# Hand-overs between the stages of a twelve-stage transformer kernel: starting at the last sum instead of the last norm

## The chip, the cores and the metric

One Trainium2 chip, one of its cores. The metric is the device time of one execution in microseconds (us), lower is better. The kernel of before ran three times: 4346.09, 4349.70 and 4349.97 us, median 4349.7. Another execution was recorded by the profiler.

## The reference, cut to what matters

A residual stream x of 2048 tokens by 256 channels (16 blocks of 128 tokens) passes twelve layers. Each computes

    x = layernorm(x + f(x))        # no scale, no shift

with another f: delta-rule attention, self attention, a spline layer, retention, quantized cross attention, a gated layer with 8-bit weights, latent attention, channel attention over a context, a ternary gated layer, a Mamba-2 scan, channel attention again, and an int8 layer. The ternary layer, whose order changes most, is

    xq = round(127 / max|n| * n) / (127 / max|n|),  n = rms_norm(x)
    p  = silu(xq @ sign(W_g).T) * (xq @ sign(W_u).T)
    f  = p @ sign(W_d).T

## The kernel before, in words

Every layer is a class (a stage), and x stays in SBUF all the time: `X` as 16 tiles of 128 tokens by 256 channels, and `xT`, its transpose, for the stages whose products need channels on the partitions. The stages are Delta, SelfAttention, Spline, Retention, Cross, Gated, Latent, Channels, Ternary, Scan, ChannelsGamma and Quant (n = 0 to 11). Tokens go through a stage in four groups of four blocks.

There is no scheduler. Each engine gets one long queue: stage after stage, and within a stage the steps that `order()` yields, so the order is written by hand. Engines meet by semaphores. `xn` counts groups whose norm has been written to X, `xt` counts halves of groups whose transpose has been kept in xT. `room[b]` names the event after which PSUM bank b is free.

A stage ends, for a group, with the sums (VectorE adds the product in PSUM to X and writes `R`), the norm (`norm_vector`: statistics L217 and L220, an inverse root in eleven small instructions L196 to L209, four scalings to X L241), the turn (`turn_tensor` L173: eight transposes on TensorE into two banks) and the copy to xT (`turn_scalar` L182, ScalarE). The norm's last scaling raises `xn`.

The next stage begins with `before(eng)` (L272), a wait for `over(n - 1)` (L188): all of xT kept if the stage in front is one that turns x (`TURNED`: Delta, Spline, Cross, Gated, Ternary), else all norms written. TensorE, ScalarE, VectorE and GpSimd call it. SelfAttention and Retention are without it on TensorE and have a step "last" in which they turn the last group of the stage in front. After it, TensorE sets all `room` to `over(n)`, so no bank is used earlier.

What the hand-overs look like on the engines:

- Cross (class at L1444): TensorE turns the context (ct), then k, v, then waits for VectorE's quantized weights (w) and rows (xq). GpSimd clears two tiles (`xVE`, L1813). VectorE: `w0`, `xq`, `v`.
- Gated (L1817): VectorE converts the weights `fgui` to `fgu` (L1905), GpSimd converts `fdni` to `fdn` in four instructions (L1929 to L1932), TensorE's first columns (L301) need `fgu`.
- Latent (L1935): TensorE multiplies weights with weights in steps "a" (L2010, four of them), then "dn" of group 0 (L307), the first step that reads xT.
- Channels (L2478): TensorE transposes the context, GpSimd makes `hXE` and `hKE` (L2693, L2696) after a small tile of VectorE (`hone`, L2634). Its last steps on VectorE are the products "mul" (L2658), behind ScalarE's copy hO (L2622). Channels can take steps of the stage behind it (`ASIDE`); before, only ChannelsGamma did this, for Quant.
- Ternary (L2714): ScalarE takes the signs of the weights (L2812, L2813). VectorE's "prep" normalizes a group, finds its largest values and rounds it to `tQB` (L2852 to L2866); then TensorE transposes (qt), and for every block u: "gu" (L2781, two banks each for gate and up), silu on ScalarE (L2826), the product on VectorE (L2873), "pt" (transposes, L2788), copies (L2831 on ScalarE, L2879 on VectorE), "dn" (L2799). In iteration t come gu of block t, pt of block t - 1, dn of block t - 2; prep of the next group at t = 1, 5, 9, sums and norm of the last one ("close") at t = 5, 9, 13, 17, the turn at t = 6, 10, 14, 18.
- Scan (L2887): TensorE multiplies dt for groups 0, 1 (n = 0) and 2, 3 (n = 1); ScalarE takes Abs of each (L3074), then Exp of each (L3078); VectorE's chain (L3141 on) follows. GpSimd builds tables (L3240 to L3257).
- ChannelsGamma (L2706): its context is loaded when the norm of Scan is over (`may_load`), because there is no room earlier.

Weights of a stage with `EARLY` are loaded one stage ahead, when `over(n - 2)` is reached.

Of the kernel before, what the change touches and what calls it, by code (L numbers as in the profile page):

```python
# [17 lines left out]
D = 256  # L18
# [227 lines left out]
class Stage:  # L246
# [926 lines left out]
class Retention(Stage):  # L1173
# [35 lines left out]

    def order(self):  # L1210
# [233 lines left out]
class Cross(Stage):  # L1444
# [37 lines left out]

    def order(self):
# [65 lines left out]
    def tensor(self, pe):  # L1549
        c, bank, room = self.c, self.c.bank, self.c.room  # L1550
        self.before(pe)
# [111 lines left out]
        for b in range(8):  # L1663
            room[b] = c.over(self.n)
# [53 lines left out]
    def vector(self, dve, own):  # L1718
        c, bank = self.c, self.c.bank
        self.before(dve)  # L1720
# [96 lines left out]
class Gated(Stage):  # L1817
# [18 lines left out]
    def buffers(self):  # L1836
# [3 lines left out]
        self.pj, self.dw, self.gs, self.hs = t("proj", 48), t("down", 4), s("silu", 24), v("h", 24)  # L1840
        self.wg, self.wd = v("w", 2), p("w", 1)

    def order(self):
# [8 lines left out]
        yield "turn", 3, 0  # L1852

    def tensor(self, pe):
        c, bank, room = self.c, self.c.bank, self.c.room
        for step, g, n in self.order():
# [11 lines left out]
            elif step == "dn":  # L1868
# [3 lines left out]
                for b in range(4):  # L1872
# [6 lines left out]
                    room[4 + b // 2] = c.xn.at(4 * self.n + g + 1)  # L1879
# [3 lines left out]
        for b in range(8):  # L1883
            room[b] = c.over(self.n)

    def scalar(self, act, own):
# [3 lines left out]
        for step, g, n in self.order():  # L1890
# [6 lines left out]
            elif step == "turn":  # L1897
                c.turn_scalar(act, self.n, g, (6, 7))

    def vector(self, dve, own):  # L1900
        c, bank = self.c, self.c.bank
        self.before(dve)
# [3 lines left out]
        for step, g, n in self.order():  # L1906
# [8 lines left out]
            elif step == "dn":  # L1915
                dve.wait_ge(*self.dw.at(g + 1))
                sums = [own(dve.tensor_tensor(c.R[:, x, :], bank(4 + x // 2)[:, blk(x % 2, 256)], c.X[:, 4 * g + x, :], ALU.add))
                        for x in range(4)]
                c.norm_vector(dve, own, self.n, g, sums)
# [15 lines left out]
class Latent(Stage):  # L1935
# [41 lines left out]

    def order(self):
# [3 lines left out]
        for step, g in shared(0):  # L1982
            yield step, g, 0, 0
        for n in range(4):
# [14 lines left out]
    def tensor(self, pe):  # L1999
        c, bank, room = self.c, self.c.bank, self.c.room  # L2000
        self.before(pe)
        pe.wait_ge(self.dma[1], 112)
        for step, g, u, e in self.order():
# [10 lines left out]
            elif step == "b":  # L2014
# [6 lines left out]
                room[2 + g] = self.bcs.at(g + 1)  # L2021
            elif step == "dn":
                if g == 0:
# [72 lines left out]
    def scalar(self, act, own):  # L2096
# [4 lines left out]
        for step, g, u, e in self.order():  # L2101
            s, gs = u % 4, g % 2
            if step == "a":
# [54 lines left out]
    def vector(self, dve, own):  # L2158
        c, bank = self.c, self.c.bank
        self.before(dve)  # L2160
# [316 lines left out]

class Channels(Stage):  # L2478
# [4 lines left out]
    PLACE, REST, GAMMA, LOADS = 57504, 80000, False, 5  # L2483
# [31 lines left out]

    def order(self):
# [16 lines left out]
    def tensor(self, pe):  # L2533
        c, bank, room = self.c, self.c.bank, self.c.room
        self.before(pe)
# [88 lines left out]
    def vector(self, dve, own):  # L2624
        c, bank = self.c, self.c.bank
        self.before(dve)
# [79 lines left out]
class ChannelsGamma(Channels):  # L2706
# [3 lines left out]
    def may_load(self, sp):  # L2710
        Stage.may_load(self, sp)


class Ternary(Stage):  # L2714


    PLACE, REST, EARLY, TURNED = 0, None, True, True

    def weights(self):
        c = self.c  # L2720
        self.gu, self.gub = c.f32("tgu", 2, 2, 1024), c.at("tgub", [128, 2, 2, 1024], BF16)
        self.dn = c.f32("tdn", 8, D)

    def load(self, sp):
        i = self.ins
        self.may_load(sp)
        cp = lambda a: a.rearrange("(c p) n -> p c n", p=128)
        self.fetch(sp, 0, (self.gu[:, 0, :, :], cp(i["t_gu"][0])), (self.gu[:, 1, :, :], cp(i["t_gu"][1])), (self.dn[:, :, :], cp(i["t_dn"])))

    def buffers(self):  # L2730
        c = self.c
        self.XN, self.s8, self.sw, self.m = (c.sets(2, "t" + n, *z) for n, *z in (("XN", 4, D), ("st", 4, 8), ("sw", 12), ("m", 12)))
        self.QB = [c.at(f"tQB{i}", [128, 4, D], BF16) for i in range(2)]
        self.QT = [c.at(f"tQT{i}", [128, 2, 512], BF16) for i in range(2)]
        self.G, self.PM, self.PT = c.sets(2, "tG", 512), c.sets(2, "tPM", 1024), c.sets(2, "tPT", 8, 128)
        t, s, v = ((lambda name, n, e=e: self.sig(e, name, n)) for e in ("tensor", "scalar", "vector"))
        self.qt, self.gm, self.um, self.pt, self.dw = t("qt", 4), t("g", 32), t("u", 32), t("pt", 32), t("dn", 16)
        self.ws, self.qtc, self.gs, self.pca = s("w", 3), s("qt", 4), s("silu", 32), s("pt", 16)
        self.iv, self.qb, self.pm, self.pcv = v("scale", 4), v("q", 4), v("p", 32), v("pt", 16)

    def order(self):
        yield "prep", 0, 0
        yield "qt", 0, 0
        for t in range(19):
            for h in range(2):
                if t < 16:
                    yield "gu", t, h
                if 0 <= t - 1 < 16:
                    yield "pt", t - 1, h
            if t % 4 == 1 and t < 12:  # L2750
                yield "prep", t // 4 + 1, 0
            if t % 4 == 3 and t < 12:
                yield "qt", t // 4 + 1, 0
            if t % 4 == 2 and t > 4:
                yield "turn", t // 4 - 1, 0
            if 0 <= t - 2 < 16:
                yield "dn", t - 2, 0
            if t % 4 == 1 and t > 4:
                yield "close", t // 4 - 1, 0

    def tensor(self, pe):
        c, bank, room = self.c, self.c.bank, self.c.room
# [695 lines left out]
```

## Time and profile before

| | before |
|---|---|
| time, median of 3 runs | 4349.7 us |
| the profiled execution | 4350.02 us, span 4348.2 us |
| TensorE busy | 3718.2 us (86%) |
| VectorE busy | 3160.9 us (73%) |
| ScalarE busy | 1977.4 us (45%) |
| GpSimd busy | 966.3 us (22%) |
| mean granted TensorE clock | 0.918 |

PE is TensorE's matmuls, PEld its weight loads, DVE VectorE, ACT ScalarE, POOL GpSimd. The span is from the first to the last instruction of the profiled execution; times in rows are counted from its start. A granted clock of 1.00 is 2.4 GHz, of 0.50 it is 1.2 GHz, and a value between is the mean of a stretch at both. In a row of instructions, "[7.04 <-DVE X L241]" says that the engine had been idle for 7.04 us and that the idle time ended with an instruction of VectorE, line 241, that writes X. With "x8" the row holds eight instructions one after the other, and the time is that of all.

### The profile page before, as it was taken

How to read it: one execution, taken by the hardware profiler on the slowest of the kernel's cores; microseconds unless marked ns; L12 is line 12 of the kernel's file. 1: busy time of each engine (PE TensorE's matmuls, PEld its weight loads, DVE VectorE, ACT ScalarE, POOL GpSimd, SP SyncE). 2: the span in 40 equal slices, each digit the busy share in tenths (PEclk: the TensorE clock that was granted, in tenths of full speed). 3: DMA queues.
4: the chain of work that ended last, by engine and by line, in shares of the span. 5: the costliest groups of instructions: out<-in, count | busy, mean ns of one | idle time of the engine just before them, and what ended most of it. 6: DMA issues, size and time to landing. Idle time of an engine off the chain costs nothing. (4 is left out here: it accounts for less than half of the span.)

```text
span 4348.2 us, 69549 instructions
## 1 busy us (share of the span) xinstructions
PE 3718.2 (86%) x25068; PEld 2252.3 (52%) x25068; DVE 3160.9 (73%) x7102; ACT 1977.4 (45%) x4701; POOL 966.3 (22%) x1237
## 2 busy tenths in 40 slices
PE   7799999998843868797999897769999999997985
PEld 3466666665522446554555554545555555554543
DVE  7789988897577665533556568558888888886678
ACT  4466666665511423212333234226556555563345
POOL 2433321354011000000111131023323233233220
PEclk9899999999965989897999989879999999997897
DMA  2222222222110000100000000200000000001000
GB/s 67 69 63 69 62 60 62 65 64 48 54 37 27 5 22 2 54 19 21 1 1 1 8 23 23 100 1 1 1 1 1 1 1 1 1 1 47 1 1 20
DMA packets 220707, 120.09 MB, mean 28 GB/s; under 512 B 115280, under 2 KB 213200, under 8 KB 219152
## 3 DMA queue, kind: packets, MB, share of 16 engines
q1 hardware_dynamic: 220368, 115.65, 9.6%
q8 instruction: 203, 3.33, 0.3%
q14 instruction: 136, 1.11, 0.1%
HBM read 100.89 MB, written 14.68 MB: 27 GB/s over the span
## 5 line engine op out<-in xcount | busy, mean ns | idle before, releaser
L301 PE MATMUL ps<-xT,min 128*128 128x512 f32 (+1 forms) x1072 | 534.8, 628 | 7.3 <-DVE mZ L3179 5.0
L3184 DVE SCALAR_TENSOR_TENSOR macc<-ps,mcw,macc 128x508 f32<-128x508 f32 (+2 forms) x408 | 302.9, 742 | 146.3 <-ACT macc L3108 136.7
L3122 ACT ACTIVATE mE<-ps,mcol 128x128 f32<-128x128 f32 x1024 | 291.3, 370 | 7.8 <-PE ps L3024 0.8
L301 PEld LDWEIGHTS ps<-xT,min 128*128 128x128 f32 (+1 forms) x1072 | 182.9, 191 | 191.1 <-issue 180.8
L3270 POOL TENSOR_TENSOR mE<-mE,mCB 128x512 f32<-128x512 f32 x128 | 163.7, 1279 | 481.5 <-ACT mE L3122 481.5
L3054 PE MATMUL ps<-mwo,macc 128*128 128x256 f32 x1024 | 246.0, 383 | 19.2 <-DVE macc L3218 19.2
L2616 ACT ACTIVATE hE<-ps 128x512 f32<-128x512 f32 x256 | 139.0, 594 | 223.2 <-PE ps L2578 223.2
L3277 POOL TENSOR_TENSOR mSQ<-mSQ,mtn 128x512 f32<-128x512 f32 x128 | 163.4, 1277 | 257.7 <-ACT mtn L3126 257.7
L2151 ACT ACTIVATE lP<-ps,lm 128x128 f32<-128x128 f32 x256 | 90.6, 366 | 266.1 <-DVE lm L2211 266.1
L3054 PEld LDWEIGHTS ps<-mwo,macc 128*128 128x128 f32 x1024 | 186.0, 191 | 47.3 <-DVE macc L3218 25.6
L2646 DVE TENSOR_REDUCE hMX<-ps 128x2 f32<-128x512 f32 x256 | 158.9, 684 | 60.2 <-PE ps L2557 60.2
L2242 POOL TENSOR_TENSOR lP<-lP,lm 128x512 f32<-128x512 f32 x64 | 66.6, 1041 | 578.3 <-DVE lm L2215 578.3
L723 DVE SCALAR_TENSOR_TENSOR dav<-ps,dsmall,dav 128x508 f32<-128x508 f32 (+2 forms) x192 | 142.4, 742 | 47.9 <-ACT dav L594 43.4
L817 POOL TENSOR_TENSOR dTB<-did,dNB 128x1024 f32<-128x1024 f32 (+1 forms) x10 | 28.7, 2866 | 663.7 <-DMA dNB<-d_N 599.5
L822 POOL TENSOR_TENSOR dTB<-dTB,dtmp 128x30 f32<-128x30 f32 (+11 forms) x300 | 169.1, 564 | 23.5
L2578 PE MATMUL ps<-hXE,hKE 32*128 32x256 f32 x1024 | 163.0, 440 | 12.7 <-DVE hXE L2652 7.2
L723 DVE SCALAR_TENSOR_TENSOR daq<-ps,dsmall,daq 128x508 f32<-128x508 f32 (+2 forms) x192 | 142.5, 742 | 39.1 <-ACT daq L594 33.6
L493 PE MATMUL ps<-dKQ 128*128 128x256 f32 x512 | 137.6, 395 | 28.6 <-ACT dO L669 19.2
L821 POOL TENSOR_TENSOR dtmp<-dNB,dTB 128x30 f32<-128x30 f32 (+11 forms) x300 | 155.2, 517 | 23.5
L723 DVE SCALAR_TENSOR_TENSOR dak<-ps,dsmall,dak 128x508 f32<-128x508 f32 (+2 forms) x192 | 142.3, 741 | 23.3 <-ACT dak L594 18.7
L3108 ACT ACTIVATE macc<-ps,ms,mcw 128x512 f32<-128x512 f32 x136 | 105.9, 779 | 115.0 <-PE ps L301 115.0
L2055 PE MATMUL ps<-lCQ,lq 128*128 128x512 f32 (+1 forms) x256 | 142.6, 656 | 17.7 <-DVE lQA L2206 17.7
(593 smaller groups left out, 8957.8 us busy)
## 6 DMA issues: line engine op xcount, KB each, us to landing
dwk<-in_L_attn_Wk SPq DMA_DIRECT2D x64, 128.0 KB, 2.3
dwq<-in_L_attn_Wq SPq DMA_DIRECT2D x64, 128.0 KB, 2.3
dwv<-in_L_attn_Wv SPq DMA_DIRECT2D x64, 128.0 KB, 2.4
dwg<-in_L_attn_Wg SPq DMA_DIRECT2D x64, 128.0 KB, 2.4
dwo<-in_L_attn_Wo SPq DMA_DIRECT2D x64, 128.0 KB, 2.6
min<-in_m_in SPq DMA_DIRECT2D x2, 4096.0 KB, 17.0
d_N<-dNT SPq DMA_DIRECT2D x256, 16.0 KB, 1.5
dTT<-d_TT SPq DMA_DIRECT2D x256, 16.0 KB, 1.9
```

The lines of the kernel that those rows point to most:

```text
L301: t = pe.matmul(out, w[:, j, :], self.c.xT[:, j, blk(g, 512)], start=j == 0, stop=j == 1)
L723: x = dve.scalar_tensor_tensor(out=acc[:, :, 3 - j:T], in0=p[:, :, 0:T - 3 + j], scalar=small[:, 4 * k + j:4 * k + j + 1], in1=acc[:, :, 3 ...
L821: then(pool.tensor_tensor(part, bc(NB[:, s, s + 1:32], s, True), bc(TB[:, s, 0:s], 31 - s), ALU.mult))
L822: then(pool.tensor_tensor(low, low, part, ALU.subtract))
L2055: t = pe.matmul(bank(b), w, self.CQ[gs][0:K, i, :], start=i == 0, stop=i == 1)
L2578: t = pe.matmul(bank(4 + i)[:, blk(lt, 256)], self.KE[x][r, e, blk(lt)], self.XE[x][r, e, :], start=True, stop=True)
L2646: m = dve.tensor_reduce(self.MX[y][:, k, 32 * r:32 * r + 32:16], bank(r).rearrange("p (e n) -> p e n", e=2), AX.X, ALU.max, negate=True)
L3054: t = pe.matmul(bank(j // 2)[:, blk(j % 2, 256)], self.acc[s][:, blk(j)], self.wo[:, i, :], start=i == 0 and j % 2 == 0, stop=i == 31 and ...
L3122: x = act.activation(self.E[s][:, e, blk(j)], bank(4 + e)[:, blk(j)], ACT.Exp, bias=self.col[:, 4 * g + j, 0, 2 * i + e:2 * i + e + 1])
L3184: x = dve.scalar_tensor_tensor(out=acc[:, :, 3 - j:T], in0=p[:, :, 0:T - 3 + j], scalar=self.cw[:, i, j:j + 1], in1=acc[:, :, 3 - j:T], op ...
L3270: pool.tensor_tensor(g4(self.E[s][:, 0, :]), g4(self.E[s][:, 0, :]), self.CB[g % 2][:, :, :], ALU.mult).then_inc(*self.m0.up)
L3277: pool.tensor_tensor(self.SQ[g % 2][:, :], self.SQ[g % 2][:, :], self.tn[s][:, :], ALU.add).then_inc(*self.sqa.up)
```

## The change

`before` waits for `ended()` of the stage in front. That is its last sums where the class says so (Retention, Cross, Gated, Latent, Channels, Ternary, Scan), else `over` as before. TensorE does not wait at all for the stage in front in Cross, Latent, Channels and Scan; VectorE waits for the norms (`xn`), not for xT.

```diff
     def before(self, eng):
-        eng.wait_ge(*self.c.over(self.n - 1))
+        eng.wait_ge(*(self.prev.ended() if self.prev else self.c.over(-1)))
...
+    def ended(self):
+        return self.c.over(self.n)
...
 class Cross / Latent / Channels / Scan
     def tensor(self, pe):
-        self.before(pe)
     def vector(self, dve, own):
-        self.before(dve)
+        dve.wait_ge(*self.c.xn.at(4 * self.n))
```

(Gated.vector has the same new wait; Scan.gpsimd has `pool.wait_ge(*c.xn.at(4 * self.n))` in place of `before`; Gated.gpsimd and Cross.gpsimd keep `before`, which is now `ended()` of Cross and of Retention.) Cross, Gated and Ternary no longer set every bank to `over`. The last group of Cross is turned by Gated, of Gated by Latent, of Ternary by Scan:

```diff
 class Cross
-                        for g in range(4):
+                        for g in range(3 if x == "turn" else 4):
...
 class Gated, order()
                 yield "h", g, n
+                if g == 0 and n == 1:
+                    yield "last", 3, 0
...
-        yield "turn", 3, 0
...
-                    room[4 + b // 2] = c.xn.at(4 * self.n + g + 1)
+                    room[4 + b // 2] = self.su.at(g + 1)
...
+            elif step == "last":
+                c.turn_tensor(pe, self.n - 1, g, (6, 7))
...
 class Latent, order()
         for step, g in shared(0):
             yield step, g, 0, 0
+            if step == "dn":
+                yield "last", 3, 0, 0
...
 class Scan, tensor() and scalar()
         for n in range(2):
+            if n:
+                c.turn_tensor(pe, self.n - 1, 3, (6, 7))
             pe.wait_ge(*room[n])
+            pe.wait_ge(*c.xt_ready(self.n, 2 * n + 1))
...
 class ChannelsGamma
     def may_load(self, sp):
-        Stage.may_load(self, sp)
+        sp.wait_ge(*self.prev.ended())
```

Ternary is moved ahead of Channels in the file, since Channels now takes two of its steps (`ASIDE = Ternary.BESIDE`), on VectorE alone. Prep is cut in two, "prep" (statistics, inverse root, scaling) and "round" (the rest), and sums and norm of a group are two steps:

```diff
+    BESIDE = {16: ("prep", 0), 17: ("round", 0)}
...
     def order(self):
-        yield "prep", 0, 0
         yield "qt", 0, 0
         for t in range(19):
             for h in range(2):
                 if t < 16:
                     yield "gu", t, h
                 if 0 <= t - 1 < 16:
                     yield "pt", t - 1, h
-            if t % 4 == 1 and t < 12:
-                yield "prep", t // 4 + 1, 0
+            if t % 4 < 2 and t < 12:
+                yield ("prep", "round")[t % 4], t // 4 + 1, 0
             if t % 4 == 3 and t < 12:
                 yield "qt", t // 4 + 1, 0
-            if t % 4 == 2 and t > 4:
+            if t % 4 == 3 and t > 4:
                 yield "turn", t // 4 - 1, 0
             if 0 <= t - 2 < 16:
                 yield "dn", t - 2, 0
             if t % 4 == 1 and t > 4:
                 yield "close", t // 4 - 1, 0
+            if t % 4 == 2 and t > 4:
+                yield "norm", t // 4 - 1, 0
...
-                room[6 + b // 2] = c.xn.at(4 * self.n + g + 1)
+                room[6 + b // 2] = self.su.at(g + 1)
             elif step == "turn":
-                c.turn_tensor(pe, self.n, u, (6, 7))
+                c.turn_tensor(pe, self.n, u, (4, 5))
...
     def scalar(self, act, own):
-        self.before(act)
         act.wait_ge(self.dma[0], 48)
         (signs of the weights)
+        self.before(act)
```

The semaphores of Channels are handed on for reuse one stage later than those of the others.

## Rows read from the trace of the kernel before

**Rows 1.** Stretches Gated, Ternary: length; busy PE, PEld, DVE, ACT, POOL; PEclk, DMA, GB/s.

```profile
1824.70:1971.80 147.10, 138.06 (x416) 72.41 (x416) 48.23 (x138) 22.15 (x33) 9.15 (x4) 0.96 0.18 53
...
2709.00:2876.30 167.30, 114.68 (x568) 86.66 (x568) 95.44 (x296) 44.38 (x62) 0.00 (x0) 0.84 0.20 79
```

**Rows 2.** Who waited for whom, Cross to Scan: us in total, times, longest.

```profile
PE ps L173 <- DVE X L241: 50.9, 6, 12.2
```

**Rows 3.** Timeline of DVE at Ternary's end: start, us, instruction, count [idle before].

```profile
2869.33 1.42 DVE L2882 TENSOR_TENSOR R<-ps,X 128x256 f32<-128x256 f32 x4 [6.22 <-PE ps L2799]
...
2874.90 1.38 DVE L241 TENSOR_SCALAR X<-R,st,rsq 128x256 f32<-128x256 f32 x4
```

**Rows 4.** Timeline at the start of Cross, POOL and PE.

```profile
1582.46 3.55 POOL L1813 MEMSET xVE<- 128x2048 f32 x2 [179.02 <-DVE X L241]
...
1594.78 1.23 PE L1539 MATMUL ps<-ident,cwr 128*128 128x128 f32 x8 [0.29 <-DVE xVE L1756]
```

**Rows 5.** Timeline at two places in Scan and Delta, DVE beside POOL.

```profile
2879.38 1.07 DVE L3167 CAST msel<-rsq 128x8 bf16<-128x8 f32 x1
...
2879.04 1.38 POOL L3240 MEMSET R<- 128x1536 bf16 x1 [206.05 <-ACT xT L182]
...
955.81 2.86 DVE L207 TENSOR_TENSOR dsw<-dsw 128x4 f32<-128x4 f32 x1
...
955.80 2.85 POOL L817 TENSOR_TENSOR dTB<-did,dNB 64x1024 f32<-64x1024 f32 x1 [23.06 <-DMA dNB<-d_N]
```

**Rows 6.** Timeline at the start of Gated, PE and POOL.

```profile
1828.40 3.72 PE L301 MATMUL ps<-xT,fgu 128*128 128x512 f32 x4 [1.69 <-DVE fgu L1905]
1832.46 26.33 PE L301 MATMUL ps<-xT,fgu 128*128 128x512 f32 x60 [0.33 <-DVE fgu L1905]
...
1827.42 4.14 POOL L1929 TENSOR_SCALAR fdn<-fdni 128x1280 f32<-128x1280 int32 x1 [241.41 <-ACT xT L182]
```

**Rows 7.** Timeline of PE at the start of Latent, and one stretch of it.

```profile
1971.86 1.97 PE L173 MATMUL ps<-ident,X 128*128 128x128 f32 x8 [7.04 <-DVE X L241]
1974.60 5.55 PE L2010 MATMUL ps<-lkvT,lqT 128*128 128x64 f32 x32 [0.77 <-ACT xT L182]
...
1974.60:1980.00 5.40, 5.40 (x32) 5.24 (x32) 0.00 (x0) 0.59 (x1) 0.00 (x0) 0.50 0.00 0
```

**Rows 8.** Timeline of POOL at the start of Channels.

```profile
2497.89 0.94 POOL L2693 TENSOR_SCALAR hXE<-X,hpar 128x256 f32<-128x256 f32 x2 [16.28 <-DVE hone L2634]
```

**Rows 9.** Timeline from Channels to Ternary, DVE, ACT and PE.

```profile
2694.32 1.75 DVE L2658 RECIPROCAL hO<-hO 128x256 f32<-128x256 f32 x1 [5.97 <-ACT hO L2622]
...
2700.63 1.75 DVE L2658 RECIPROCAL hO<-hO 128x256 f32<-128x256 f32 x1 [3.64 <-ACT hO L2622]
...
2718.29 0.69 DVE L2866 TENSOR_SCALAR tQB<-tXN 128x1024 bf16<-128x1024 f32 x1
...
2708.99 3.71 ACT L2812 ACTIVATE tgub<-tgu 128x2048 bf16<-128x2048 f32 x2 [8.39 <-DVE X L241]
...
2721.24 5.22 PE L2781 MATMUL ps<-tgub,tQT 128*128 128x512 bf16 x12 [1.10 <-ACT tQT L2820]
```

**Rows 10.** Timeline inside Ternary, PE and DVE; L2781 begins an iteration.

```profile
2747.84 1.03 PE L2781 MATMUL ps<-tgub,tQT 128*128 128x512 bf16 x4
...
2774.90 1.94 PE L173 MATMUL ps<-ident,X 128*128 128x128 f32 x8 [12.19 <-DVE X L241]
...
2788.84 1.03 PE L2781 MATMUL ps<-tgub,tQT 128*128 128x512 bf16 x4
...
2794.89 1.03 PE L2781 MATMUL ps<-tgub,tQT 128*128 128x512 bf16 x4
...
2755.30 0.75 DVE L2873 SCALAR_TENSOR_TENSOR tPM<-ps,tm,tG 128x512 f32<-128x512 f32 x1 [3.35 <-PE ps L2781]
```

**Rows 11.** Timeline of ACT at the start of Scan, the second Abs.

```profile
2884.87 0.69 ACT L3074 ACTIVATE mCB<-ps,mh 128x512 f32<-128x512 f32 x1 [1.33 <-PE ps L301]
```

**Rows 12.** Timeline of DVE at the start of ChannelsGamma.

```profile
3991.74 0.23 DVE L2629 TENSOR_REDUCE hrow<-ident 128x1 f32<-128x4 f32 x2 [4.42 <-DMA hctx<-in_ctx]
```

More of the change, by code:

```diff
@@ L1208, in buffers, with ended @@
         self.vz = p("v_zero", 1)
+    def ended(self):
+        return self.sm.at(8)
     def order(self):
@@ L1481, in buffers, with ended @@
         self.vz = p("v_zero", 1)
+    def ended(self):
+        return self.sum.at(4)
     def order(self):
@@ L1662, in tensor @@
                 c.turn_tensor(pe, self.n, g, (0, 1))
-        for b in range(8):
-            room[b] = c.over(self.n)
     def scalar(self, act, own):
@@ L1840, in buffers, with ended @@
         self.pj, self.dw, self.gs, self.hs = t("proj", 48), t("down", 4), s("silu", 24), v("h", 24)
+        self.su = v("sum", 4)
         self.wg, self.wd = v("w", 2), p("w", 1)
+    def ended(self):
+        return self.su.at(4)
     def order(self):
@@ L1882, in tensor @@
                 c.turn_tensor(pe, self.n, g, (6, 7))
-        for b in range(8):
-            room[b] = c.over(self.n)
+            elif step == "last":
+                c.turn_tensor(pe, self.n - 1, g, (6, 7))
     def scalar(self, act, own):
@@ L1898, in scalar @@
                 c.turn_scalar(act, self.n, g, (6, 7))
+            elif step == "last":
+                c.turn_scalar(act, self.n - 1, g, (6, 7))
     def vector(self, dve, own):
         c, bank = self.c, self.c.bank
-        self.before(dve)
+        dve.wait_ge(*self.c.xn.at(4 * self.n))
         dve.wait_ge(self.dma[0], 96)
@@ L1916, in vector @@
                 dve.wait_ge(*self.dw.at(g + 1))
-                sums = [own(dve.tensor_tensor(c.R[:, x, :], bank(4 + x // 2)[:, blk(x % 2, 256)], c.X[:, 4 * g + x, :], ALU.add))
-                        for x in range(4)]
-                c.norm_vector(dve, own, self.n, g, sums)
+                for x in range(4):
+                    o = dve.tensor_tensor(c.R[:, x, :], bank(4 + x // 2)[:, blk(x % 2, 256)], c.X[:, 4 * g + x, :], ALU.add)
+                o.then_inc(*self.su.up)
+                dve.wait_ge(*self.su.at(g + 1))
+                c.norm_vector(dve, own, self.n, g, [0] * 4)
     def gpsimd(self, pool, own):
@@ L1976, in buffers, with ended @@
         self.pn = p("pn", 64)
+    def ended(self):
+        return self.su.at(4)
     def order(self):
@@ L2000, in tensor @@
         c, bank, room = self.c, self.c.bank, self.c.room
-        self.before(pe)
         pe.wait_ge(self.dma[1], 112)
@@ L2021, in tensor @@
                 room[2 + g] = self.bcs.at(g + 1)
+            elif step == "last":
+                c.turn_tensor(pe, self.n - 1, g, (4, 5))
             elif step == "dn":
+                pe.wait_ge(*c.xt_ready(self.n, g))
                 if g == 0:
@@ L2102, in scalar @@
             s, gs = u % 4, g % 2
+            if step == "last":
+                c.turn_scalar(act, self.n - 1, g, (4, 5))
+                continue
             if step == "a":
@@ L2159, in vector @@
         c, bank = self.c, self.c.bank
-        self.before(dve)
+        dve.wait_ge(*self.c.xn.at(4 * self.n))
         dve.wait_ge(self.dma[0], 48)
@@ L2478 @@
 class Channels(Stage):
-    PLACE, REST, GAMMA, LOADS = 57504, 80000, False, 5
+    PLACE, REST, GAMMA, LOADS, ASIDE = 57504, 80000, False, 5, Ternary.BESIDE
     def weights(self):
@@ L2514, in buffers, with ended @@
         self.xe, self.ke, self.ve = p("xe", 16), p("ke", 16), p("ve", 16)
+    def ended(self):
+        return self.sum.at(16)
     def order(self):
@@ L2625, in vector @@
         c, bank = self.c, self.c.bank
-        self.before(dve)
+        dve.wait_ge(*self.c.xn.at(4 * self.n))
         dve.wait_ge(self.dma[0], 32)
@@ L2936, in buffers, with ended @@
         self.sq0, self.m0, self.sqa = p("sq0", 4), p("m", 128), p("sq", 128)
+    def ended(self):
+        return self.summed.at(4)
     def order(self):
@@ L3072, in scalar @@
         for n in range(2):
+            if n:
+                c.turn_scalar(act, self.n - 1, 3, (6, 7))
             act.wait_ge(*self.dm.at(n + 1))
@@ L3129, in vector @@
         c, bank = self.c, self.c.bank
-        self.before(dve)
+        dve.wait_ge(*self.c.xn.at(4 * self.n))
         dve.wait_ge(self.dma[0], 80)
@@ L3238, in gpsimd @@
         c = self.c
-        self.before(pool)
+        pool.wait_ge(*c.xn.at(4 * self.n))
         zero = own(pool.memset(self.spread[:, :, :, :, :], 0.0))
@@ L3288, in program @@
             stages.append(kind(core, n))
-            if not stages[n].ASIDE:
-                core.hand_on(stages[n])
+            for m in (n - 1, n):
+                if m >= 0 and bool(stages[m].ASIDE) == (m < n):
+                    core.hand_on(stages[m])
         with nc.Block() as block:
```

322 lines of the change are left out of this document (168 added, 154 removed).

## The prediction

> **What bounds the kernel now.** I read the table by stage first: TensorE is busy 94% of Gated and 69% of Ternary [rows 1]. So most of the time is TensorE's own work, which the change leaves alone; what it can win lies where TensorE stands still. The list of waits gives the common cause: the turns of x (L173) waited 50.9 us in six waits for the norm (L241), the longest 12.2 us [rows 2]. A hand-over is a chain: the sums end, the norm follows, then the turn, its copy, and the next stage. From the end of the last sums of Ternary (2870.75) to the end of the norm (2876.28) it is 5.5 us [rows 3]; call that one norm. Times are start us, and the engine at each one must be asked what it waited for *last*.
>
> **Retention to Cross.** TensorE, ScalarE and the two memsets of xVE begin one norm earlier. But VectorE's own chain (its norm, w0, xq, then v) runs unbroken into the turn of the weights, which waited for xVE, 0.29 us [rows 4]: TensorE's early start wins 0. The memsets do not come free. Rows of two other places show GpSimd holding up VectorE: a CAST of 8 elements took 1.07 us and ended with a memset, and a 4-element product took 2.86 us beside a GpSimd instruction of 2.85 us [rows 5]. The memsets, 3.55 us from 1576.8 on, now lie on the norm, whose small tensor_scalars come at 1578.6, as the second one starts: +1.75 us (bounds 0 and 1.8).
>
> **Cross to Gated.** Undisturbed, VectorE converts fgu right after the norm (1824.7 instead of 1827.36), so the first columns start at 1825.8 instead of 1828.40; the last turn, about 1 us at full speed, now lies inside a stage where TensorE is full: -3 + 1 = -2.0. But GpSimd's four instructions (9.15 us busy, some of it waiting [rows 1]; 4.14 us the first [rows 6]) also start one norm earlier, at 1817.86, just behind the bias add, and then alternate with the norm's small instructions. GpSimd, 7.7 us without its waits, ends at 1827.3; VectorE still owes the products and the scaling, 3 us: norm end at 1830.3 instead of 1824.68. Columns start at 1831.3, the second group (at half clock the first takes 3.72) at 1835.0 instead of 1832.46 [rows 6]: +2.5, and +1.0 for the turn: **+3.5 us**. Bounds -2.0 (GpSimd never blocks) and +5.5 (the clock rises later too). The Trainium skill (SBUF, State Buffer, section Who interferes with whom) has the rule that speaks against this move: the shared ports are a lock, and the later of the two engines blocks entirely. These rows agree; by it the sum stays as it is.
>
> **Gated to Latent.** TensorE idled 7.04 us before the turn at 1971.86, so it was free at 1964.8; the products "a" (two runs like the one shown, 11 us) began at 1974.60 [rows 7], then dn(0). Both read loaded weights and x turned earlier, so after the change "a" starts at 1964.8: -9.8 us. The last turn falls after dn(0), where TensorE waits for VectorE anyway: 0. Further, "a" ran at a granted clock of 0.50 [rows 7] behind the idle time; now it follows full-clock work with no gap. If it stayed full, "a" would take 5.5: another 5.5 saved. But the same row shows TensorE busy for all of 5.4 us with the clock not rising, so this narrow work (64 columns) does not hold the clock well; I take half, 2.7. **-12.5 us**, bounds -9.8 and -15.3. By the Trainium skill (TensorE: Matmul & The Clock Gate, section The HAM clock gate), what counts is how busy the engine has been, and "a" would stay full throughout; the rows at 0.50 speak against it.
>
> **Latent to Channels.** The first scores wait for GpSimd's hXE, which waits for VectorE's hone [rows 8], behind the norm as before. 0 (bounds 0.3 either way).
>
> **Channels to Ternary.** VectorE does prep and round of group 0 inside Channels. Prep is statistics, root and scaling, as the norm: 5.6 us; both end 10.0 us after the norm (2708.96 to 2718.98) [rows 9], so round is 4.4. Prep fits the idle 5.97 us, round has 3.64 us [rows 9]: norm end +0.7, at 2709.7. The signs (3.71 us, and 1.9 for tdn) start at 2700.6 behind the last hO; tQT is copied by 2707.3; columns start at 2707.4 instead of 2721.24 [rows 9]: -13.8.
>
> **Inside Ternary.** One iteration at full speed is 6.05 us; four were 41.0 (2747.84 to 2788.84), since prep, sums and norm (17 us on VectorE) stood in one block and the turn waited 12.19 us [rows 10]. Per iteration VectorE owes two products (0.75 [rows 10]) and a copy, 2.0 us, so it can spend 4.0 more before it falls behind, and TensorE runs one iteration ahead. In three blocks (prep 5.6; round and sums 5.8; norm 5.6) I get, from the start A of the iteration with prep: VectorE done at A+9.6, then A+17.4, while dn of the next group, due at A+14.7, waits for those sums: 2.7 lost. The turn is due at A+23.9; its first bank waits for the qt copy, the second, bank 5, for the copy of pt behind the norm, A+26.9: 2.6 lost beside 1.7 of turn and qt. 24.2 + 2.7 + 2.6 + 1.3 = 30.8, and 0.9 for a clock that sags in such gaps: 31.7 instead of 41.0, twice: -18.6. In the first four iterations prep costs 3.5 instead of 5.5, with the clock -2.0. After the last group's sums the norm stalls 2.6 instead of 4.5 (with the clock, -3.5). **Ternary in all -37.9**; bounds -13.8 (the hand-over alone) and -43 (no stall left).
>
> **Ternary to Scan.** dt of groups 0, 1 runs before the turn and Abs(0) after the sums. Abs(1) then stands where Abs(0) stood, so what lies between them goes: 1.33 + 0.69 [rows 11] = **-2.0** (bounds -1.0, and -2.7, the turn with its copy). GpSimd's tables come earlier by the same.
>
> **Scan to ChannelsGamma.** The context is fetched from the sums on, not the norm; VectorE idled 4.42 us for it [rows 12]. It lands before the norm ends: **-4.4**. SP has Quant's loads behind it, also earlier, not needed for 40 us. Loads of Latent wait for the moved turn in Gated, some us later, 130 us ahead of need: 0. The semaphores handed on later cost nothing.
>
> **Sum.** 1.75 + 3.5 - 12.5 + 0 - 37.9 - 2.0 - 4.4 = -51.6. The profiled execution took 4350.02 us (span 4348.2), 0.3 above the median of 4349.7, so the sum is made on it and carries over: **4298.5 us**. A measurement of this kernel tells about 0.2% (9 us) from no change.
>
> **Rivals.**
> - *The ports do not bite*: no loss at the first two hand-overs, -7.3 more: 4291. For: the norm's instructions are short and could slip between. Against: rows 5. 0.13.
> - *The clock stays full through "a"* (the page's rule, as a mechanism of this kernel): the remaining 2.8 go too: 4295.7. 0.08.
> - *Ternary wins its hand-over only*: VectorE's total work is unchanged, and the three blocks just spread the same stall: -13.8 instead of -37.9: 4322.6. For: 5.6 is over the 4.0 free. Against: TensorE's lead of one iteration. 0.12.
> - *Slower*: in Ternary the short gaps, now several per group, keep the clock at its lower level throughout. An iteration is then 12.1 us; 16 of them with the tail 198.6, so dn ends at 2906 instead of 2869.3: +36.7, against -13.7 elsewhere: 4373. It decides from 10.7 us an iteration on. Against: behind a gap of 12.19 us the second iteration is back at 6.05 [rows 10]. 0.03.
> - *The waits are not what holds TensorE*: each stage start meets another wait ending at the same time, as in Latent to Channels; 4350. 0.04.
>
> The forecast itself: 0.60, own range 4284 to 4312. The range goes down to just under the sum of the good bounds (-67.2: 4283), since what follows "a" could gain from the clock too, and up to 4318, short of the third rival, which with the last two leaves out 0.19. Faster by over 0.2%: 0.60 + 0.13 + 0.08 + 0.12 and what the last two keep, 0.94; within: 0.03; slower: 0.03.
>
> **What would show it.** In the profile after: fgu's conversion ends about 5 us after its old time within Cross to Gated, and small VectorE instructions there of 0.6 to 3 us (if 0.17, the first rival). No idle before "a", and its granted clock. Ternary: the waits of L173 for L241 under 3 us each, and 31 to 32 us for four iterations (41: third rival). Abs(0) ahead of the turn in Scan; no DMA wait at ChannelsGamma. The prediction is wrong if Ternary, from norm end to norm end, is shortened by under 25 us, or if a stage between the hand-overs changes length.

## The result and the profile after

The changed kernel took 4299.57 us (median of three runs, 4298.24 to 4302.71) against 4349.7; the ratio is 0.989, 95% interval 0.987 to 0.991. The forecast was 4298.5. Run again beside other kernels it took 4289.5 (median of four, 4286.66 to 4297.01) against 4349.46, ratio 0.986 (0.985 to 0.988). So the change is worth some 50 to 60 us, and a total of this kernel moves by several us from run to run. That is why the experiments below are read in the trace first, stage by stage, and in their totals only second.

The profiled executions took 4350.02 before and 4302.71 after (span 4300.9). Line numbers in rows are those of the kernel that the row comes from, so the same statement has another number before the change, after it and in an experiment. The stretches of Gated and of Ternary, the columns as in [rows 1]:

```profile
1836.60:1975.10 138.50, 137.43 (x417) 72.22 (x417) 38.80 (x110) 22.06 (x33) 0.00 (x0) 0.98 0.18 56
2705.10:2828.80 123.70, 110.96 (x553) 84.10 (x559) 80.17 (x239) 38.47 (x59) 0.00 (x0) 0.93 0.28 106
```

These are the stretches in which TensorE works on the stage: it is busy for 99% of Gated's and 90% of Ternary's. Both start and end at other points of the hand-over than [rows 1] do. The waits of the turns over the same stretch as [rows 2]:

```profile
PE ps L173 <- DVE X L241: 6.2, 2, 5.3
...
PE ps L173 <- ACT tQT L2615: 2.4, 2, 1.2
```

Of 50.9 us in six waits for the norm 6.2 in two are left, the longer at the turn that Scan takes over; two short ones have another releaser, the copy of tQT.

**Retention to Cross** answers to [rows 4] (the timeline of VectorE, GpSimd and TensorE):

```profile
1582.43 1.75 DVE L196 TENSOR_SCALAR rsq<-st 128x4 f32<-128x4 f32 x1
...
1580.60 3.56 POOL L1820 MEMSET xVE<- 128x2048 f32 x2 [173.13 <-DVE rR L1434]
...
1600.16 1.94 PE L1549 MATMUL ps<-ident,cwr 128*128 128x128 f32 x8 [11.29 <-DVE xVE L1763]
1601.90 1.91 PE L1549 MATMUL ps<-ident,xXA 128*128 128x128 f32 x8
```

One instruction on 4 elements takes 1.75 us beside the two memsets and ends with the second of them. The norm is 1.6 us longer (from the scaling of the group before to this one 10.51 us, before the change 8.92). And the turn of the weights, behind 11.29 us of idle TensorE, takes 1.94 us where it took 1.23.

**Cross to Gated**, [rows 6]:

```profile
1828.26 1.45 DVE L196 TENSOR_SCALAR rsq<-st 128x4 f32<-128x4 f32 x1
...
1830.72 2.80 DVE L209 SCALAR_TENSOR_TENSOR rsq<-rsq 128x4 f32<-128x4 f32 x1
1833.56 0.65 DVE L205 SCALAR_TENSOR_TENSOR rsq<-rsq 128x4 f32<-128x4 f32 x1
...
1836.63 1.70 DVE L1919 TENSOR_SCALAR fgu<-fgui 128x1408 f32<-128x1408 int32 x2
...
1825.21 4.47 POOL L1945 TENSOR_SCALAR fdn<-fdni 128x1280 f32<-128x1280 int32 x1 [241.05 <-DVE R L1805]
...
1830.63 2.88 POOL L1947 TENSOR_TENSOR fdn<-fdn,fsd 128x1280 f32<-128x1280 f32 x1
```

From one norm's scaling to the next (1818.59 to 1835.22) it takes 16.63 us, before 12.04: +4.6. The 4.6 lie in the norm itself: from the bias add in front of it (L1809) to the scaling it takes 10.1 us in all ten profiles with GpSimd early, 5.5 before the change. The three long instructions of VectorE end within 0.1 us of instructions of GpSimd. Against that the conversion of fgu now stands right behind the norm and the turn lies inside Gated: the next norm comes 51.34 us later, before 52.82: -1.5.

**Gated to Latent**, [rows 7]. TensorE without a gap from Gated's last products (L1889) through "a" (L2030), dn(0) and the turn, and the clock of the stretch:

```profile
1963.16 11.97 PE L1889 MATMUL ps<-fdn,fH 128*128 128x256 f32 x48
1975.07 6.08 PE L2030 MATMUL ps<-lkvT,lqT 128*128 128x64 f32 x64
1981.08 3.72 PE L311 MATMUL ps<-ldn,xT 128*128 128x256 f32 x16
1984.63 1.04 PE L173 MATMUL ps<-ident,X 128*128 128x128 f32 x8
...
1960.00:1980.00 20.00, 20.00 (x110) 14.58 (x109) 5.23 (x21) 2.92 (x5) 0.00 (x0) 1.00 0.00 1
```

"a" takes 6.08 us at a granted clock of 1.00, where it ran 11.05 us at 0.50, and dn(0) 3.72 where it took 5.38.

**Channels to Ternary and inside it**, [rows 9, 10]:

```profile
2705.30 1.38 DVE L241 TENSOR_SCALAR X<-hR,st,rsq 128x256 f32<-128x256 f32 x4
...
2705.09 4.83 PE L2578 MATMUL ps<-tgub,tQT 128*128 128x512 bf16 x11 [6.85 <-ACT tQT L2615]
...
2746.36 5.41 PE L2596 MATMUL ps<-tdn,tPT 128*128 128x256 f32 x16 [2.30 <-DVE R L2694]
...
2756.01 1.06 PE L173 MATMUL ps<-ident,X 128*128 128x128 f32 x8 [1.19 <-ACT tQT L2615]
...
2752.37 1.38 DVE L241 TENSOR_SCALAR X<-R,st,rsq 128x256 f32<-128x256 f32 x4
...
2783.56 1.38 DVE L241 TENSOR_SCALAR X<-R,st,rsq 128x256 f32<-128x256 f32 x4
```

The columns (L2578) start 0.2 us ahead of the norm's scaling instead of 13.7 behind it. The distance of the two norms is four iterations, 31.2 us: four times 6.05, the wait of dn for the sums (2.3), the lower clock behind it (this dn takes 5.41 us, the others 3.62), the turn's wait (1.19), and qt and the turn themselves.

**At Scan and at ChannelsGamma**, [rows 11, 12]:

```profile
2842.49 0.69 ACT L3133 ACTIVATE mCB<-ps,mh 128x512 f32<-128x512 f32 x1 [3.87 <-PE ps L305]
...
3945.66 1.38 DVE L241 TENSOR_SCALAR X<-R,st,rsq 128x256 f32<-128x256 f32 x4
3947.07 0.23 DVE L2854 TENSOR_REDUCE hrow<-ident 128x1 f32<-128x4 f32 x2
```

The second Abs comes 7.9 us behind the start of the scaling (10.0 before), and hrow follows the norm with no wait for a transfer.

### The profile page after: what moved, and what is told of

Read it like the earlier page. It is cut to its first block, busy times and chain, and to the rows that moved or that the text cites. A ratio compares the mean times of both kernels' runs of the same rounds, so it can differ in the third digit from the quotient of the medians.

```text
span 4300.9 us, 69538 instructions
## 1 busy us (share of the span) xinstructions
PE 3705.8 (86%) x25052; PEld 2244.1 (52%) x25068; DVE 3159.7 (73%) x7102; ACT 1976.4 (46%) x4701; POOL 968.1 (23%) x1237
## 4 chain that ended last, share of the span: by engine, by line
PE 61%; DVE 24%; issue 5%; ACT 5%; POOL 3%; SPq 1%; DMA 1%; DVEq 0%; ACTq 0%; POOLq 0%
PE ps L305 20%; PE ps L3111 5%; PE ps L2078 3%; PE ps L2803 3%; PE ps L3099 3%; PE ps L2816 2%; PE ps L2782 2%; PE ps L497 2%; PE ps L2113 1%; POOL dTB L826 1%; PE ps L2596 1%; PE ps L575 1%; DVE macc L3243 1%; POOL dtmp L825 1%; DVE hMX L2871 1%
```

## The experiments

Each is an edit of the changed kernel. "Norm to norm" is the time between the starts of two scalings (L241) of VectorE; it leaves out what happened earlier in the run. Each kernel has one profile (the changed one has two), so a reading counts most where many kernels share the code.

**GpSimd late.**

```diff
 # Cross
-        self.before(pool)
+        pool.wait_ge(*self.c.xn.at(4 * self.n))
 # Gated
-        self.before(pool)
+        pool.wait_ge(*self.wg.at(2))
```

> The changed kernel, but GpSimd's memsets in Cross wait for Retention's last norm again, and its four instructions in Gated wait until VectorE has converted fgu. Theory (GpSimd holds up VectorE's short instructions): the norm before Cross loses its one instruction of 1.75 us (1.6 us saved), the norm before Gated takes some 4.6 us less and the conversion of fgu stays right behind it; together -6.2 us on 4299.6, so 4293.4, less if the later memsets are waited for in Cross. Rival (those long instructions are something else's fault, or TensorE would wait anyway): 4299.6, with instructions of over 1 us still inside the two norms.

4282.5 us (five runs, 4276.0 to 4294.8), ratio 0.984 (0.983 to 0.985). Its profile:

```profile
1587.13 1.38 DVE L241 TENSOR_SCALAR X<-rR,st,rsq 128x256 f32<-128x256 f32 x4
...
1588.57 3.55 POOL L1820 MEMSET xVE<- 128x2048 f32 x2 [178.77 <-DVE X L241]
...
1820.94 1.38 DVE L241 TENSOR_SCALAR X<-R,st,rsq 128x256 f32<-128x256 f32 x4
...
1832.98 1.38 DVE L241 TENSOR_SCALAR X<-R,st,rsq 128x256 f32<-128x256 f32 x4
1834.40 1.70 DVE L1919 TENSOR_SCALAR fgu<-fgui 128x1408 f32<-128x1408 int32 x2
```

Retention's norm is back at 8.92 us, Cross's at 12.04: 1.6 and 4.6 us, and xVE was still ready 13.76 us behind the norm, as in the changed kernel. 0.6 of it goes again in Gated, so 5.6 stay of the 6.2 forecast. GpSimd is the cause: both long norms are gone when it starts late. Not all of it is kept in Cross here: the products behind the turn of the weights (L1597) ran 5.78 us instead of 3.67, and the first scores came 2.1 us later than in the changed kernel. The total fell by more than 5.6 (17 us against the first set of the changed kernel, 7 against the second; forecast 4293.4). The surplus is not explained; the largest difference beside the two norms is Latent's first part, 6.2 us shorter in the profile (below).

**TensorE late in Cross.**

```diff
 # Cross.tensor
+        pe.wait_ge(*self.c.xn.at(4 * self.n))
         pe.wait_ge(self.dma[0], 112)
```

> The changed kernel, but TensorE waits for Retention's last norm again before its first product in Cross. Theory (starting early on work that VectorE's chain ends later anyway only leaves TensorE idle behind it, and the turn of the weights and the first scores then run at the lower clock): the turn of the weights runs at full clock (1.2 and 1.0 us instead of 1.9 and 1.9) and Cross loses some 2 us: 4297.6. Rival (the clock of that stretch is chance, VectorE's chain alone counts): 4299.6, at most 0.3 us away in the profile.

4295.3 us (4293.32 to 4298.58), ratio 0.987 (0.986 to 0.989). The turn of the weights and what follows:

```profile
1597.63 1.23 PE L1549 MATMUL ps<-ident,cwr 128*128 128x128 f32 x8 [1.01 <-DVE xVE L1764]
1598.69 1.04 PE L1549 MATMUL ps<-ident,xXA 128*128 128x128 f32 x8
```

Full clock again, and from this turn to the first scores 8.5 us instead of 9.9. So the first scores lose 1.4 us by the early start: TensorE finished its first products early, stood idle and was slow at the one point that everything waits for. All profiles say the same: 8.5 us in the four in which TensorE starts late here (the kernel before, this one and the two under "All together"), 9.9 in the nine with an early start and the same memsets, 12.0 in pool_late. Whether the 1.4 us reach the end of the stage isn't shown: from Retention's last norm to Cross's third the four late ones take 230.2 to 230.3 us, the nine early ones anything from 226.3 to 233.7 (mean 229.6) with identical code.

**Latent: start and clock apart.** Both kernels hold "a" until Gated's last norm; the second is busy meanwhile.

```diff
 # Latent.tensor, latent_cold
+        pe.wait_ge(*self.c.xn.at(4 * self.n))
         pe.wait_ge(self.dma[1], 112)
 # latent_warm, in front of that wait
+        pe.wait_ge(*room[0])
+        for _ in range(52):
+            pe.transpose(bank(0)[:, blk(0)], c.ident[:, :], c.ident[:, :])
```

> The changed kernel, but TensorE waits in Latent for Gated's last norm before the products 'a'. Theory (start and clock both count): 'a' starts 7.2 us later and, behind the idle time, runs at a granted clock of 0.5 in 11.5 us instead of 6.1, dn(0) in 5.4 instead of 3.7: +7.2 + 5.4 + 1.7 = +14.3, so 4313.9. Rival (only the start counts): +7.2, 4306.8.

> As latent_cold, with 52 turns of the identity matrix into a free bank ahead of the wait, so that TensorE is busy (some 6.8 us) while the norm runs, and starts 'a' just as late. Theory (the clock is kept by what ran in front): 'a' in 6.1 us at a granted clock of 1.00, dn(0) in 3.7: +7.2 to +7.6, so 4307. Rival (the narrow products of 'a' do not hold the clock, it falls inside them): as latent_cold, 4313.9.

Cold 4307.8 us (4297.91 to 4315.47), ratio 0.990 (0.988 to 0.992); warm 4300.1 (4293.1 to 4302.65), 0.988 (0.987 to 0.989). TensorE in the cold kernel, and its clock:

```profile
1974.40 11.08 PE L2031 MATMUL ps<-lkvT,lqT 128*128 128x64 f32 x64 [7.16 <-DVE X L241]
1985.41 5.06 PE L311 MATMUL ps<-ldn,xT 128*128 128x256 f32 x16
...
1980.00:1986.00 6.00, 6.00 (x33) 5.68 (x34) 0.00 (x0) 1.65 (x3) 0.00 (x0) 0.50 0.01 3
```

and in the warm one:

```profile
1972.34 5.89 PE L2024 MATMUL ps<-ident 128*128 128x128 f32 x52
1979.58 6.08 PE L2034 MATMUL ps<-lkvT,lqT 128*128 128x64 f32 x64 [1.34 <-DVE X L241]
...
1980.00:1986.00 6.00, 6.00 (x65) 5.70 (x64) 0.00 (x0) 2.06 (x4) 0.00 (x0) 1.00 0.01 3
```

From the end of Gated's last products to the turn of lCN it takes 16.7 us in the changed kernel, 24.0 warm, 30.3 cold. So starting early is worth 7.2, and the kept clock 6.3: 5.0 in "a", 1.3 in dn(0). Both are shown in the trace. The totals alone would not have decided it: cold was forecast at 4313.9 and its rival (only the start counts) at 4306.8, nearer the 4307.8 measured. The rival of the warm kernel (narrow products let the clock fall) is refuted for the 6.08 us that they last: the same 64 products hold full clock when full-clock work ends 1.34 us ahead of them, and don't raise it in 11 us behind 7.16 us of idle time. Whether they would hold it for longer isn't shown. By the Trainium skill ("TensorE: Matmul & The Clock Gate", section The HAM clock gate) the clock follows how busy the engine has been; the warm kernel agrees, the 11 us busy at 0.50 in the cold one don't fit it.

**Ternary: the old order inside.** Prep and round in one block, sums and norm in one, the turn an iteration earlier; all hand-overs as changed.

```diff
 # Ternary.order
-            if t % 4 < 2 and t < 12:
-                yield ("prep", "round")[t % 4], t // 4 + 1, 0
+            if t % 4 == 1 and t < 12:
+                yield "prep", t // 4 + 1, 0
+                yield "round", t // 4 + 1, 0
...
-            if t % 4 == 3 and t > 4:
+            if t % 4 == 2 and 4 < t < 18:
                 yield "turn", t // 4 - 1, 0
...
                 yield "close", t // 4 - 1, 0
-            if t % 4 == 2 and t > 4:
                 yield "norm", t // 4 - 1, 0
```

> The changed kernel with the old order inside Ternary (prep and round together, sums and norm together, turn in the third iteration), all hand-overs as changed. Theory (the three rounds have a gain of their own): four iterations take 41.0 us again instead of 31.2, twice, and some 2 to 3 us more around the first and last group: +22, so 4321.6. Rival (only the hand-over counts, the three rounds spread the same stall): 4299.6, four iterations at 31 us in both.

4318.05 us (4314.49 to 4319.02), ratio 0.993 (0.991 to 0.995).

```profile
2787.87 1.11 PE L173 MATMUL ps<-ident,X 128*128 128x128 f32 x4 [12.23 <-DVE X L241]
2789.78 1.12 PE L173 MATMUL ps<-ident,X 128*128 128x128 f32 x4 [0.80 <-DVE tPT L2688]
```

The wait of 12.2 us of [rows 10] is back, and four iterations take 42.1 us from norm to norm (41.0 expected). From Channels' last norm to Ternary's last it is 156.2 us, against 129.3 changed and 167.3 before. The three rounds win 26.9 of the 38.0, so the rival is refuted. The total (4321.6 expected) is 18.5 above the first set of the changed kernel and 28.5 above the second.

**Group 0 behind the norm.**

```diff
 # Ternary
-    BESIDE = {16: ("prep", 0), 17: ("round", 0)}
+    BESIDE = {}
...
     def order(self):
+        yield "prep", 0, 0
+        yield "round", 0, 0
         yield "qt", 0, 0
```

> The changed kernel, but prep and round of group 0 stay behind Channels' last norm in Ternary instead of beside Channels' last blocks. Theory: the columns start 13.7 us behind the norm's scaling as before the change instead of 0.2 us ahead of it: +13.9; Channels' tail wins 0 to 0.7 back: 4313.2. Rival (prep and round beside Channels cost its tail the 3.3 us that the profiled pair shows): the last norm comes 3.3 us nearer to the third one: 4310.2.

4308.6 us (4307.23 to 4309.35), ratio 0.991 (0.989 to 0.993). Norm to norm over Ternary 143.5 us, 14.2 more; the columns start at 2711.93, 14.0 behind the scaling. Channels' last two norms lie 20.60 us apart here and 20.61 before the change. With prep and round beside they lie 21.12 us apart in seven profiles, 23.93 in four profiles (both of the changed kernel among them) and 27.40 in one (cross_pe). So against the changed kernel this one wins 3.3 us, as the rival said, and its total lies nearer the rival's 4310.2 than the theory's 4313.2. I put 0.5 us down to prep and round, and the rest to the clock. It is below full speed in all profiles just before the third norm, ahead of prep, and differs in how long it stays down: over the 6 us from this norm on it was granted 0.87 in this kernel, 0.89 in latent_cold (21.12 us), 0.63 in the changed kernel and 0.50 in cross_pe. That prep and round have no part in the longer ones isn't shown, since neither kernel without them has one.

**A better order in Ternary.** The sums ahead of round (close_first), and besides the turn behind dn (close_turn).

```diff
 # Ternary.order
-            if t % 4 < 2 and t < 12:
-                yield ("prep", "round")[t % 4], t // 4 + 1, 0
+            if t % 4 == 0 and t < 12:
+                yield "prep", t // 4 + 1, 0
...
                 yield "close", t // 4 - 1, 0
+            if t % 4 == 1 and t < 12:
+                yield "round", t // 4 + 1, 0
 # close_turn besides
-            if t % 4 == 3 and t > 4:
-                yield "turn", t // 4 - 1, 0
             if 0 <= t - 2 < 16:
                 yield "dn", t - 2, 0
+            if t % 4 == 3 and t > 4:
+                yield "turn", t // 4 - 1, 0
```

> The changed kernel, but VectorE takes the sums of a group before round instead of behind it. Theory (dn of the next group waits 2.3 us for those sums, and TensorE's clock then takes 1.8 us more of it): both go, twice, 8.2 us less, of which the products behind round take up to 1.5 us each back: 4293, four iterations in 28 to 29 us instead of 31.2. Rival (VectorE's work is the bound, the wait moves to the products): 4299.6, four iterations in 31 us.

> As close_first, and the turn of x moves behind dn of its iteration. Theory (the turn waits 1.19 us for the copy of tQT, the last one 0.9 + 1.3 us for the norm and the copy of tPT; behind dn both are done): 3 to 4 us less than close_first: 4289.5. Rival (behind dn the copies of the turn hold banks 4 and 5 from the next turn of the products): as close_first.

close_first took 4291.6 us (4289.22 to 4298.25), ratio 0.987 (0.986 to 0.989), close_turn 4275.0 (4271.49 to 4285.55), 0.984 (0.982 to 0.986). The total of close_first lies at its forecast (4293), but by luck: the mechanism was wrong. TensorE in it:

```profile
2740.99 1.12 PE L173 MATMUL ps<-ident,X 128*128 128x128 f32 x4 [3.99 <-DVE X L241]
2742.90 1.12 PE L173 MATMUL ps<-ident,X 128*128 128x128 f32 x4 [0.80 <-DVE tPT L2690]
2743.81 5.39 PE L2598 MATMUL ps<-tdn,tPT 128*128 128x256 f32 x16
```

dn no longer waits for the sums and stays fast, so TensorE comes to the turn 4.1 us sooner, but the norm, behind round as ever, does not: the wait has moved to the turn (3.99 + 0.80), the slow dn comes behind it, and four iterations take 33.5 us instead of 28 to 29. Ternary is 2.8 us longer than in the changed kernel, so nothing of the total's fall against the first set of the changed kernel comes from here. Neither theory nor rival had named the turn. In close_turn the turn has dn in front of it, and waits 0.48 and 1.26:

```profile
2751.21 0.66 PE L173 MATMUL ps<-ident,X 128*128 128x128 f32 x4 [0.48 <-DVE X L241]
2753.13 0.66 PE L173 MATMUL ps<-ident,X 128*128 128x128 f32 x4 [1.26 <-DVE tPT L2690]
```

Four iterations take 29.6 us and Ternary 120.6, 8.7 less than in the changed kernel. Against close_first it is 11.5 less where 3 to 4 were expected (in total 16.6), because close_first itself had gone wrong.

**The changed kernel again, and the fetch of ChannelsGamma.**

```diff
 # ChannelsGamma.may_load
-        sp.wait_ge(*self.prev.ended())
+        sp.wait_ge(*self.c.over(self.n - 1))
```

> The changed kernel itself once more, with more runs, beside the others of this call. Theory: 4299.6, within 4 us; where its stages of unchanged code differ from the first profile (Retention's end to Cross's third norm, Latent, the tail of Channels: up to 6 us between the kernels tried so far whose code there is identical), the difference lies in the granted clock. Rival (the early start of the stages puts those losses in every run): the same stage times as in the first profile, within 0.5 us.

> The changed kernel, but the context of ChannelsGamma is fetched behind Scan's last norm again instead of its last sums. Theory (VectorE's first instruction of the stage waits for this transfer): it waits 4.4 us again, and the first scores come 4.4 us later behind the norm: 4304.0. Rival (TensorE meets another wait there): the same distance from the norm to the first scores as in the changed kernel, 4.8 us: 4299.6.

The fetch: 4290.5 us (4282.8 to 4296.47), ratio 0.986 (0.984 to 0.988). VectorE waits again:

```profile
3933.93 0.23 DVE L2854 TENSOR_REDUCE hrow<-ident 128x1 f32<-128x4 f32 x2 [4.34 <-DMA hctx<-in_ctx]
```

The first scores come 9.1 us behind the scaling, 4.8 in the changed kernel: 4.3 as expected. The total (4304.0 expected) is 1 us from that of the changed kernel beside it; 4 us can't be seen in it.

The changed kernel again shows why. Its 4289.5 us lie 10 below the first set, outside the 4 that I had expected. Its profiled execution is 5.7 us shorter than the first; from Cross's first norm to Scan's second (1690 us) it repeats the first to 0.2 us, apart from one fixed shift of 2.1. So most stages repeat exactly, as the rival said (the tail of Channels too, 23.9 us both times), and the differences are a few jumps: between Retention's last norm and Cross's first 3.4 us, inside Scan 2.9. Latent shows them best: from Gated's last norm to Latent's first, the profiles of kernels with identical code there show 231.2 us (four), 226.9 (four), 226.3 (two) or 225.0 (one). The last three are of kernels in which GpSimd starts late in Gated, the stage in front; whether that has a part in it isn't shown. 231.2 and 226.9 both occur with the same code in both stages. The changed kernel (first row) and pool_late, the one at 225.0 (second), over the same part of it:

```profile
2040.00:2060.00 20.00, 17.70 (x73) 9.89 (x71) 10.16 (x20) 7.53 (x29) 3.12 (x3) 0.74 0.00 1
```

```profile
2038.00:2058.00 20.00, 17.70 (x93) 10.09 (x92) 11.45 (x23) 9.82 (x39) 3.71 (x4) 0.91 0.01 2
```

The same 17.70 us busy hold 73 matmuls at a granted clock of 0.74 and 93 at 0.91.

**All together.** GpSimd late, TensorE late in Cross, close_turn's order; the second kernel moves the turn one iteration further.

```diff
 # together_next, Ternary.order, behind dn
-            if t % 4 == 3 and t > 4:
-                yield "turn", t // 4 - 1, 0
+            if t % 4 == 0 and t > 4:
+                yield "turn", t // 4 - 2, 0
```

> Four edits on the changed kernel: GpSimd late in Cross and Gated, TensorE late in Cross, and in Ternary sums ahead of round and the turn behind dn. Theory (their gains lie at different places and add up): 5.6 at the two norms, 1.4 at the turn of the weights, 8.7 in Ternary by the profiles, 15.7 in all: 4283.9 or less, with the clock's chance 4268 to 4286. Rival (one undoes another: later memsets and later TensorE meet in Cross): the turn of the weights waits 1 us more, 4285.

> As together_late, but the turn of x in Ternary moves one iteration further, behind dn of the first iteration of the next group. Theory (there the norm and the copy of tPT are long done, so the turn waits for nothing, and the clock stays full): four iterations in 25.5 to 26 us instead of 29.6, 4 us less, twice, less 0.3 for products that wait for the copy of the turn: 7 us below together_late. Rival (VectorE with 23.4 us of work per group is the bound): 28 us or more, 2 us below together_late.

4268.1 us (4265.86 to 4277.56), ratio 0.981 (0.980 to 0.983), and 4271.6 (4266.57 to 4279.54), 0.982 (0.980 to 0.984): both beat the changed kernel beside them (0.986, 0.985 to 0.988) and the kernel before. By stages the first was to take 4283.9 or less, and 4268 to 4286 with the clock's chance; it came out at the lower end. In Cross the weights' turn (1594.86) waits 0.28 us for xVE and runs at full clock, as in [rows 4], and the norm before Gated takes 12.07 us. In the second one the turn in Ternary (at 2738.71) waits for nothing:

```profile
2738.71 1.04 PE L173 MATMUL ps<-ident,X 128*128 128x128 f32 x8
...
2731.00:2757.60 26.60, 25.73 (x143) 19.98 (x145) 23.34 (x75) 9.45 (x15) 0.00 (x0) 1.00 0.00 1
```

Four iterations take 26.6 us (29.6 in the first, 25.5 to 26 expected) and Ternary 116.4 (121.2 in the first): 4.8 less, where 7 were expected. Yet the totals show none of it, the second is 3.5 us higher within overlapping ranges: Scan took 1104.4 us in the first and 1111.1 in the second, with the same code. Its length is 1104.4 in two of the profiles, 1107.6 to 1108.6 in seven and 1111.1 in four of the changed code, and 1111.05 before the change.

## Why the prediction was right, and where it was not

The sum was -51.6. Read in the trace at each hand-over, the parts below come to about -54, and the two measured differences are -50.1 and -59.9; that the first stands 1 us from the forecast is partly luck. Outside the parts, stages that the change leaves alone came out otherwise in the profile of the changed kernel, by the clock as far as the trace shows: Cross up to its third norm was 0.5 us longer beyond the 1.4 named below, Channels' last group 2.8 beyond the price of prep and round. The prediction had named such a change of length between the hand-overs as a sign that it is wrong, and had no term for it.

- *Retention to Cross*, +1.75. The memsets cost 1.6, and pool_late takes it away; the rows of two other places had shown it ahead. Missed: +1.4 at the weights' turn, seen up to the first scores. The step "TensorE's early start wins 0" asked only what it waits for and not at which clock it would then run.
- *Cross to Gated*, +3.5. Measured +4.6 - 1.5 = +3.1; without GpSimd's early start 0 and -0.9 in pool_late (-2.6 in the last two kernels), so the rival "the ports do not bite" is refuted, 5.6 us in all. Short instructions of VectorE wait for long ones of GpSimd (1.45, 2.80, 0.65 us), as forecast. The Trainium skill (SBUF, State Buffer, section Who interferes with whom) has VectorE and GpSimd exclude each other at shared ports for a whole instruction; the trace agrees, in that the three end with GpSimd's.
- *Gated to Latent*, -12.5. This step failed: norm to the turn of lCN 11.0 us instead of 27.6, so **-16.6**. The start gave its 9.8, the clock 5.0 in "a"; I had taken half of 5.5, on the ground that "this narrow work (64 columns) does not hold the clock well". The row at 0.50 showed that this work doesn't *raise* the clock; that it would not *hold* it doesn't follow, and the warm kernel shows that it does. Besides, dn(0) behind it won 1.7 (1.3 against latent_cold), which the sum left out. The rival, whose part of 2.8 was to go too, was the better reading.
- *Latent to Channels*, 0: +0.35.
- *Channels to Ternary*, -13.8: -13.9 by the columns against the norm, and undoing it costs 14.2. Prep and round cost the norm 0.5 (0.7 forecast), with the reservation above.
- *Inside Ternary*: 31.2 us for four iterations (31.7 forecast). Of the two waits the first was right (2.3 for the sums, 2.7 forecast). The second was the wrong one: bank 5 was free, the turn waited for the copy of tQT in bank 4, 1.19 instead of 2.6; the clock took 1.8 instead of 0.9; and turn and qt take 1.7, as the prediction's own text says, where its sum has 1.3. The errors cancel. By the starts of the iterations the first four win 2.5 (2.0 forecast), the next eight 19.4 (18.6), what follows 2.3 (3.5). Ternary in all, with the hand-over: -38.0 from norm to norm (forecast -37.9), and -37.5 with the 0.5 that the norm in front loses.
- *Ternary to Scan*, -2.0: the second Abs against the norm -2.1, the first product of the next step -2.2. Inside Scan the gain can't be followed further, since its length jumps by more.
- *Scan to ChannelsGamma*, -4.4: -4.4, by the wait that went, and 4.3 when it is undone.

One slip moves nothing: the best bounds add up to -67.4, with Latent's 0.3 to -67.7, and not to -67.2.

## What to carry to other kernels

Moving a stage's start ahead moves its side work too: what GpSimd or TensorE then does early should be asked for its price, in VectorE's short instructions and in the clock at the point that everything waits for, and held back where it wins nothing. When one wait is taken out, ask at once what the next instruction of that engine will wait for: here the wait for the sums moved to the turn (3.99 + 0.80 us), and only with the turn behind dn, and then one iteration further, did it go (four iterations in 31.2, 33.5, 29.6 and 26.6 us). And read a change of 5 us in the profile, from norm to norm, since in a kernel of 4300 us the total doesn't show it.

## What the runs showed that I had not expected

The lengths of unchanged stages take a few values that come again (Latent's first part 225.0 to 231.2 us, Scan 1104.4 to 1111.1, Channels' last group 21.1, 23.9 or 27.4 us), with the granted clock as the visible difference, and most of the rest repeats within 0.2 us. By the Trainium skill ("TensorE: Matmul & The Clock Gate", section The HAM clock gate) the slow stretch of one kernel differs from run to run; the two profiles of the changed kernel agree (Scan 1111.1 and 1108.1 us with the same code). What sets the value in a given run is open; it wasn't tried.

From Retention's last norm to Cross's third, the four profiles with TensorE late in Cross gave 230.2 to 230.3 us, the nine with it early 226.3 to 233.7. So an early start may cost steadiness as well, but four profiles are few for that.

And 64 products of 64 columns ran 11.08 us at a granted clock of 0.50 with TensorE busy throughout, yet 6.08 us at 1.00 when work at full clock stood in front of them.
